# Decoder block on one core: values projected by row tile, output weights halved after the first turn, and a new order at the feed-forward seams

## What is computed

```python
x = x + attn(layernorm(x))        # 16 query heads, 4 key/value heads of 128; each head normed, rotary, causal
x = x + xattn(layernorm(x), ctx)  # 32 heads of 16; q and k normed; 361 context rows for each batch
x = x + ffn(layernorm(x))         # silu(x Wu') * (x Wg') Wd', the weights reduced to {-1,0,1} * scale
```

## Time and profile before

| | us |
|---|---|
| median of 3 runs (lowest, highest) | 1337.52 (1336.99, 1341.01) |
| the profiled execution | 1341.33 |
| its span, first to last instruction | 1338.3 |
| PE (TensorE) busy in the span | 1297.4 (97%) |
| VectorE, ScalarE, GpSimd busy | 754.0, 640.3, 299.0 |
| mean granted TensorE clock | 0.996 |

### The profile page before, as it was taken

The page is one execution under the profiler, slowest core; times in us unless marked ns, Lnnn a source line. Parts: engine busy times, 40 slices in busy tenths (PEclk is TensorE's granted clock), DMA queues, the critical chain, the costliest instruction groups (busy, mean ns, idle before and its releaser), DMA issues.

```text
span 1338.3 us, 27069 instructions
## 1 busy us (share of the span) xinstructions
PE 1297.4 (97%) x10812; PEld 865.0 (65%) x10812; DVE 754.0 (56%) x1813; ACT 640.3 (48%) x1451; POOL 299.0 (22%) x281
## 2 busy tenths in 40 slices
PE   8989999999999999999999999999999899999998
PEld 7656666667666666566666666666666565555554
DVE  6887767777677776343444334545445883444423
ACT  4843344333533346376766776666565323222322
POOL 0853344443334451111101110111101121000000
PEclk9999999999999999999999999999999899999999
DMA  7300000000000003122222222001012300000000
GB/s 307 142 1 1 1 1 1 1 1 1 1 1 1 1 2 139 70 72 71 71 71 71 71 71 87 24 24 55 25 55 95 127 33 24 0 24 1 24 1 29
DMA packets 22892, 60.11 MB, mean 45 GB/s; under 512 B 1584, under 2 KB 11312, under 8 KB 19568
## 3 DMA queue, kind: packets, MB, share of 16 engines
q1 hardware_dynamic: 22768, 58.39, 12.3%
HBM read 55.11 MB, written 3.28 MB: 44 GB/s over the span
## 4 chain that ended last, share of the span: by engine, by line
PE 92%; DVE 3%; issue 2%; ACT 2%; POOL 0%; DVEq 0%; POOLq 0%; ACTq 0%
PE A L1711 19%; PE C L2059 12%; PE A L1615 12%; PE A L1674 10%; PE C L1742 6%; PE B L1759 5%; PE A L2078 4%; PE C L1643 3%; PE C L1658 3%; PE A L1624 3%; PE A L1692 3%; PE B L2078 2%; PE B L1635 2%; PE B L1728 2%; PE B L1651 2%
## 5 line engine op out<-in xcount | busy, mean ns | idle before, releaser
L1711 PE MATMUL A<-wxhl,arena 128*122 128x512 f16 x1152 | 265.6, 381 | 0.0
L1711 PEld LDWEIGHTS A<-wxhl,arena 128*122 128x122 f16 x1152 | 149.7, 134 | 88.7 <-issue 8.3
L1615 PE MATMUL A<-arena,wxhl 128*125 128x512 f16 (+1 forms) x780 | 173.1, 379 | 0.0
L534 POOL TENSOR_TENSOR arena<-arena,region 122x512 f32<-122x512 f32 (+2 forms) x61 | 62.9, 1061 | 414.1 <-DVE region L1169 414.1
L763 ACT ACTIVATE arena<-C 122x1600 f32<-122x1600 f32 x96 | 144.4, 1504 | 15.4 <-PE C L1742 15.4
L1615 PEld LDWEIGHTS A<-arena,wxhl 128*125 128x125 f16 (+1 forms) x780 | 104.4, 136 | 58.4 <-DVE arena L1292 0.4
L2059 PE MATMUL C<-arena 128*128 128x375 f16 (+1 forms) x768 | 138.8, 333 | 0.0
L509 POOL TENSOR_TENSOR region<-tub 125x512 f32<-125x512 f32 (+1 forms) x65 | 82.6, 1271 | 232.0 <-DVE tub L1038 232.0
L679 ACT ACTIVATE region<-C,negm 100x100 f32<-100x100 f32 x256 | 84.2, 356 | 93.6 <-DVE negm L1081 93.5
L1674 PE MATMUL A<-arena,stageb 128*125 128x512 f16 (+1 forms) x416 | 123.8, 379 | 0.7 <-ACT arena L747 0.7
L2059 PEld LDWEIGHTS C<-arena 128*128 128x128 bf16 x768 | 74.8, 97 | 58.8
(11 more groups left out here) (182 smaller groups left out, 2226.1 us busy)
## 6 DMA issues: line engine op xcount, KB each, us to landing
stageb<-in_wffn SPq DMA_DIRECT2D x16, 768.0 KB, 4.8
arena<-in_ctxt SPq DMA_DIRECT2D x16, 722.0 KB, 6.0
stageb<-in_wffn SPq DMA_DIRECT2D x8, 1024.0 KB, 6.1
arena<-in_wqkv SPq DMA_DIRECT2D x4, 1024.0 KB, 11.9
wxhl<-in_wffn SPq DMA_DIRECT2D x4, 1024.0 KB, 4.7
arena<-in_wx SPq DMA_DIRECT2D x3, 1024.0 KB, 6.9
out_x<-xres SPq DMA_DIRECT2D x12, 224.0 KB
xres<-in_x SPq DMA_DIRECT2D x1, 2560.0 KB, 12.6
```

The lines of the kernel that those rows point to most:

```text
L534: pool.tensor_tensor(t, t, r, ALU.mult).then_inc(sig[done], 1)
L1615: ins = pe.matmul(A[j % 2][0:m, :], xp[:, k, at:at + m], wp[:, j, k, :], start=(n == 0), stop=(n == 11))
L1711: ins = pe.matmul(A[(par + n) % 2][0:KC, :], xp[:, k, c * KC:(c + 1) * KC], wp[:, 1 if n < 4 else 2, k, :], start=(i == 0), stop=(i == 11))
```

## The change

1. The values are projected by tile, in the thirteen turns or starts that project a tile, with up to 125 rows. ScalarE copies them to `vt`, and SyncE copies the rows with one or two DMAs from there to `vvs[b % 2]` of their batch (`vt` and the second buffer lie where rotary tables and gains lay). The three attention-only turns have no value projection any more.
2. Output weights 6 and 7 are staged in tiles 5 to 12 of the residual `xres`, with no wait; those tiles of x are loaded when GpSimd has halved both (`g_wlo` 4). Before turn 0 GpSimd now halves 5 and 8 alone. 6 and 7 follow at the end of turn 0. `w_hi(9)` moves from after group 2 to after group 0 of turn 0, `w_lo(9)` from after group 3 to after group 2, `next_stats(0)` to the start of the groups. Two of five `z` scalings of tile 1 go to ScalarE.
3. In the last cross turn PE does `up_gate(0, 0)` (into banks A) and `up_gate(0, 1)` beside the last two `attend2`; VectorE does `hidden(0, 0)` there, and the table load for Silu goes behind `out_back` 2.
4. In a unit, `add_ffn(u - 1)` stands ahead of `hidden(u, 0)`; `hidden(u, e + 1)` ahead of the ternaries of e; `row_scales3` is cut into four parts for e = 9 to 12; all `normed3` are at e = 13; after unit 0, `x3_lo` 1 stands behind `hidden_lo(u, 15)`.

```diff
-        ostage = [stage[:, 0], stage[:, 1], wstage[4], alo[:, :].rearrange("p (k n) -> p k n", k=KT)]
+        ostage = [xres[:, 5:9], xres[:, 9:13], wstage[4], alo[:, :].rearrange("p (k n) -> p k n", k=KT)]
...
+            sp.wait_ge(d_tab, 10)
+            for i in range(TL):
+                sp.wait_ge(*count("a_v", i, 1))
+                for b, lo, hi, at in pieces(i):
+                    sp.wait_ge(*count("pe_av", b - 2, 4))
+                    sp.dma_start(vvs[b % 2][lo:hi], vt[at:at + hi - lo]).then_inc(ld_v[b % 2], 16)
+                if i == 1:
+                    sp.wait_ge(g_wlo, 4)
+                    sp.dma_start(xres[:, 5:TL, :], x[:, 5:TL, :]).then_inc(ld_x2, 16)
...
 # GpSimd, before turn 0, and at the end of turn 0
-            w_lo(6, 2)
-            w_lo(8, 3)
-            w_lo(7, 4)
+            w_lo(8, 2)
...
+                if b == 0:
+                    for j in (0, 2, 4):
+                        z_of(1, j, 2 if j else 1)
+                    w_lo(6, 3)
+                    w_lo(7, 4)
+                    return
...
 # ScalarE
+            def v_of(i):
+                n = rows_of(i)
+                act.wait_ge(*count("pe_v", i, 1))
+                if i > 0:
+                    for landed, total in landed_values(i - 1):
+                        act.wait_ge(landed, total)
+                act.activation(vt[0:n], A[1][0:n, :], ACT.Copy, scale=1.0 / (SX * SW)).then_inc(sig["a_v"], 1)
...
                 for g in range(4):
                     a_hi(b, g)
-                v_of(b + 1)
+                if new:
+                    v_of(new[0][0])
+                if b == 0:
+                    z_part(1, 1)
+                    z_part(1, 3)
                 if new and x_tile(b) is not None:
                     x_hi(x_tile(b), A[1])
+                if b == 0:
+                    for j in (6, 7):
+                        w_hi(j)
+                        w_scaled(j)
...
 # VectorE, turn and unit
+                if b == 0:
+                    next_stats(0)
                 for g in range(4):
                     proj(*new[g])
                     sums(b, g)
-                    if b == 0 and g == 3:
+                    if b == 0 and g == 2:
                         w_lo(9)
...
             def unit(u, first=False, last=False):
-                hidden(u, 0)
                 if not first:
                     add_ffn(u - 1)
+                    hidden(u, 0)
...
 # PE, attention_only
                 p_turn(b, 0, B[1])
-                if x is not None:
-                    pe.wait_ge(*count("d_xlo", x, 1))
-                else:
-                    pe.wait_ge(*count("a_v", b, 1))
-                values_of(b + 1)
                 pe.wait_ge(*count("d_zT", i, 5))
                 p_turn(b, 1, B[0])
...
 # PE, last cross turn
                 if end < 2:
                     scores2(b + 1, 0)
+                else:
+                    up_gate(0, 0, True)
                 attend2(b, 3, par)
                 if end == 2:
+                    pe.wait_ge(*count("a_e", b, NU))
+                    up_gate(0, 1, True)
                     pe.wait_ge(*count("d_on", o2_tile(b), 1))
```

More of the change, by code:

```diff
@@ L347, in build @@
         ld_g = sem("ld_g")
-        ld_x1 = sem("ld_x1")
+        ld_x1, ld_x2 = sem("ld_x1"), sem("ld_x2")
         ld_x0 = sem("ld_x0")
+        ld_v = [sem(f"ld_v{n}") for n in range(2)]
         ld_x = sem("ld_x")
@@ L411, in build, with landed_values, landed_batch @@
         block = ctx.enter_context(nc.Block())
+        def landed_values(i):
+            n = [0, 0]
+            for t in range(i + 1):
+                for b, _, _, _ in pieces(t):
+                    n[b % 2] += 16
+            return list(zip(ld_v, n))
+        def landed_batch(b):
+            return ld_v[b % 2], 16 * sum(c == b or (c < b and c % 2 == b % 2) for t in range(TL) for c, _, _, _ in pieces(t))
         @block.sync
@@ L916, in turn @@
                 exp2(b, 5)
-                if end == 2:
-                    act.activation(fsc[:, 15:16], cst[:, C_ONE:C_ONE + 1], ACT.Silu)
                 if end < 2:
@@ L922, in turn @@
                 out_back(b, 2)
+                if end == 2:
+                    act.activation(fsc[:, 15:16], cst[:, C_ONE:C_ONE + 1], ACT.Silu)
                 if end < 1:
@@ L1220, in row_stats3, with scales3_part @@
                     st.did(dve.bn_stats(stats3[0:n, r], xres[0:n, i, :]))
-            def row_scales3(u):
+            def scales3_part(u, part):
+                t = len(unit_tiles(u))
+                if part > 0:
+                    if part == 1:
+                        rsqrt_start(rs3[:, 0:t], ms3[:, 0:t])
+                    st.chain(rsqrt_step(rs3[:, 0:t], ms3[:, 0:t], t))
+                    return
                 st.wait()
-                t = len(unit_tiles(u))
                 st.did(dve.tensor_copy(statc3[:, 0:t], stats3[:, 0:t]))
@@ L1232, in row_scales3 @@
                 st.chain(dve.tensor_scalar(ms3[:, 0:t], mv3[:, 0:t, 1], EPS_LN, SX ** -2, ALU.add, ALU.mult))
-                st.chain(rsqrt(rs3[:, 0:t], ms3[:, 0:t], t))
+            def row_scales3(u):
+                for part in range(4):
+                    scales3_part(u, part)
             def normed3(u, r):
@@ L1408, in _ @@
             dve.wait_ge(ld_x, 16)
-            for b in range(1, NB - 1):
+            turn(1)
+            turn(2)
+            dve.wait_ge(ld_x2, 16)
+            for b in range(3, NB - 1):
                 turn(b)
@@ L1506, in turn @@
                     add_cross(o2_tile(b), 1)
-                if end == 2:
-                    ternary(5, 1)
-            for b in range(NB):
-                turn(b, b % 2, max(0, b - NB + 3))
             def hidden(u, e):
@@ L1548, in unit @@
             def unit(u, first=False, last=False):
-                hidden(u, 0)
                 if not first:
                     add_ffn(u - 1)
+                    hidden(u, 0)
+                tiles = [] if last else range(len(unit_tiles(u + 1)))
                 for e in range(ET):
@@ L2085, in unit @@
             def unit(u, first=False, last=False):
-                up_gate(u, 0, first)
+                if not first:
+                    up_gate(u, 0)
                 for e in range(ET):
-                    if e + 1 < ET:
+                    if e + 1 < ET and not (first and e == 0):
                         up_gate(u, e + 1, first)
@@ L2097, in unit @@
                     down(u, e, first)
-            pe.wait_ge(*count("a_e", NB - 1, NU))
+            for b in range(NB):
+                turn(b, b % 2, max(0, b - NB + 3))
             pe.wait_ge(*count("a_o", NB - 1, NT))
```

155 lines of the change are left out of this document (77 added, 78 removed).

## The result

The changed kernel takes 1330.16 us (median of 6 runs, 1328.81 to 1331.25), beside 1338.60 us for the kernel before on the same chip (6 runs, 1336.99 to 1341.12). The ratio is 0.9927, with a 95% interval of 0.9916 to 0.9939: about 8.4 us less. Forecast were 1328.4 us and 9.1 less. The profiled execution took 1328.81 us, with a span of 1327.0.

What follows compares the result with a forecast made beforehand. PE, holding 92% of the chain that ended last, was taken to bound the kernel. From a median of 1337.52, -5.2 + 8.9 - 6.6 - 6.2 = -9.1 gave 1328.4 us; own range 1325 to 1332, eight in ten 1317 to 1332.

Steps and rivals of the forecast that it cites:

- The forecast case: End of turn 0: table operations caught by both GpSimd subtractions, PE waits 7.7 us, clock falls; 1328.4 us, chance 0.55.
- Part 1: Attention-only turns: three value projections go, each saving 2.59 us less 0.85 returned as a `z_back` 4 wait; -5.2 us.
- rival (c): Values' trip through `vt`: `attend` waits for late copies in 12 turns, +36 us, time about 1354; chance 0.03.
- (a): End of turn 0: all table operations get through before `w_lo(6)`; sum -19.3, time 1318.2 us, chance 0.24.
- Part 2, turn 0: Turn 0: moved `w_lo(9)` replaces the `p_turn` 2 wait by three of 0.7 to 0.8; turn 1 begins earlier, -1.3 us.
- Part 2, the end of turn 0: Caught table operations delay `row_max`; PE waits +7.7 us before turn 1's third projection, then a low clock costs +2.5.
- The picture of whole-instruction exclusion: VectorE operations with two SBUF inputs and GpSimd operations exclude each other whole and alternate; a 4.1 us subtraction blocks fully.
- (b): End of turn 0: one table operation alone caught, by `w_lo(6)`; PE waits 3.2 us, sum -16.1, time 1321.4, chance 0.13.
- the seam's clock: Before the feed-forward part: low clock, 0.51 for 5.1 us, lost 2.5 us; the same loss assumed at turn 0's end.
- Part 3: Seam before the feed-forward part: new PE order removes waits; -6.6 us, 2.5 of it clock; ends -4.1 and -7.6.
- Part 4: Feed-forward part: seven `down` waits go, three at `row_scales3`, three at `down(u, 0)`, one of 0.4; -6.2 us.
- The sum: Whole kernel: -5.2 + 8.9 - 6.6 - 6.2 = -9.1 us, giving a forecast median of 1328.4 us.

Runs made afterwards that it cites:

- e3_fill: Changed kernel with 26 unread matmuls filling PE's 7.18 us wait before the third projection of turn 1; 1328.31 us.
- e1_order: Changed kernel with one added wait: GpSimd starts its two subtractions at the end of turn 0 only after all four table operations; 1321.17 us.
- e11_one: Changed kernel with one added wait: GpSimd waits for the first two of four table operations before its subtractions at the end of turn 0; 1325.88 us.
- e6_add: Changed kernel with `hidden(u, 0)` put back ahead of `add_ffn(u - 1)` in three units; 1333.04 us.
- e9_seam_all: Changed kernel with the whole seam edit undone: old PE and VectorE order, and the Silu table load back before `out_back` 2; 1334.44 us.
- e5_seam: Changed kernel with the seam's old PE and VectorE order restored, but the Silu table load left in its new place; 1334.68 us.

## Why the prediction was right

**The forecast case came.** Table operations of VectorE caught by GpSimd's two subtractions, a wait of PE before the third projection of turn 1 and a low clock behind it, and twice as much gained at the three other places. 1328.4 was forecast, 1330.2 measured, 0.13% apart. The mechanism held step by step. That the numbers lie so close is in part luck: the clock behind the meeting cost less than was put down, the seam gave less by the medians, and the two errors offset each other.

**Part 1** (-5.2, that is 1.74 a turn): 1.71 to 1.96 between the kernels (0.24 of the 1.96 lies ahead of that turn's `p_turn` 0), 1.72 put back. That the next operation would wait 0.85 for `z_back` 4 was the step that mattered; `p_turn` 1 now starts 202.59 - 201.41 = 1.18 us behind `p_turn` 0 instead of 0.35, that is 0.83 later. The trip through `vt` is nowhere among PE's waits, so rival (c) had nothing. Its 1354 was also 36 us on top of (a) and not on top of the forecast, which would be 1364.

**Part 2, turn 0** (-1.3): -1.19. The waits were 0.54, 0.58 and 0.67 for the 0.7, 0.8 and 0.7 of the text, and none stood at `p_turn` 2.

**Part 2, the end of turn 0** (+7.7 and +2.5): +7.34 and +1.55. The picture of whole-instruction exclusion was right in each step: the table operations started 6.8, 7.1 and 7.4 us behind `normed` (76.98), GpSimd at 7.4 (7.2 to 7.3 in the text), the wait for a whole subtraction was 4.3, and the second was caught because the two engines alternate. The term that was mis-sized is the clock: the loss at the seam was taken over whole, and here it was 1.55 in this profile, 1.50 by e3_fill, and at most 2.1 in the eight profiles. The Trainium skill's rule (SBUF — State Buffer, "Who interferes with whom") holds for a 4.1 us instruction: the waiting operation was stretched by the full length, two times. It says that whoever issues first gets the port. GpSimd starts 0.03 us ahead of the third operation in five profiles, and in four of them it had the first turn and in one VectorE had it, so the start times of the trace don't tell which was first at that distance.

**The rivals** (a) and (b) were real and close. The 0.24 and 0.13 given to them describe a margin of 0.5 us, but the outcome of the third operation hung on a distance that the trace does not resolve (0.03 to 0.05 us between the starts). That two were caught, and not one, the prediction could not know. Ten profiles have the meeting as the change leaves it, and in one the third operation got through. Their prices were too large: (a) was to gain 19.3 us, and e1_order, which makes that outcome the rule, gains 18.0 on the kernel before on its chip; (b) was to gain 16.1, and e11_one gains 13.4. Both sums carried the 2.5 of the seam's clock whole. Up to `p_turn` 0 of turn 1, e1_order lost 0.70 us on the kernel before where (a) had nothing, 0.20 of it the wait for `p_of` behind the later low halves, and e11_one lost 3.50 where (b) had 3.2.

**Part 3** (-6.6): -6.41 between the two profiles, and so it looked confirmed. The experiments show that it is not one number. The order gives 3.5 (the text had 4.1), and the clock 0 in one profile and 2.9 in another; over the runs of a group it comes to 4.8. The lower end, -4.1, was nearer to the middle than the value taken. The new place of the Silu table's load, which the text didn't price, is worth nothing in the new order.

**Part 4** (-6.2): -6.08. The three waits for `add_ffn` were right (1.23, 1.23 and 0.83 us before, the same in e6_add, whose stretch is 3.6 longer). The three for `row_scales3` were right as differences between the kernels, but not as the price of the pieces: without them unit 0 would have got 1.7 worse.

**The sum** promised 0.7 more than came. By the two profiles the parts are worth 11.3 less the 1.0 of the start, 10.3; the medians show 8.4. A cause that fits is the seam's clock, low in the profiled run of the kernel before and not in that of e9_seam_all; single runs without a profile can't show it.

## What to carry to other kernels

Where two engines exclude each other by whole instructions, a short operation costs as much as the longest operation of the other engine that it can meet; look for the places where the one has a long chain to its first use and the other a long operation that nobody awaits, and write the order down with a wait (one added wait was worth 8 us here, as much as the whole change). A stage that ends in such a meeting has more than one time, so one profile of it is one draw. And when an experiment undoes a part of a change, compare the stretch with the kernel before, wait by wait: e5_seam came out at 14.45 us and not 16.75, about half of it because one moved instruction on another engine had been forgotten, and the rest because the clock fell less.

## What was not expected of the hardware

- With GpSimd's start 0.03 us ahead in the trace the meeting went one way in four profiles and the other way in a fifth, 5.4 us apart at PE.
- The granted clock did not answer to PE's gaps alone. Behind waits of 2.29, 0.54 and 0.96 us it was 0.51 in one execution and 1.00 in another; behind the unfilled 7.18 us the two projections took 6.89 to 7.50 us in all eight profiles that have it, and behind 3.29 us they took 5.39 in both.
- VectorE's `row_max`, with its large input in PSUM, kept its 0.52 us an operation beside a subtraction of GpSimd that stretched operations with two inputs in SBUF from 0.42 to 4.3.
